# One GpSimd chain for the factors of both normalisations, and the residual's moments ahead of the first remainder

## The reference, cut to what matters

```python
x = x + attn(layernorm(x))     # linear attention with decay in 4 heads; attn returns its input + reads @ W_read.T
x = x + ffn(layernorm(x))      # 8 experts, the best 2 for each token, F = 1024, gelu

def layernorm(x):              # without gain and offset
    m, v = mean(x, -1), var(x, -1)
    return (x - m) / sqrt(v + 1e-5)
```

## Time and profile before

| | us |
|---|---|
| median of 3 runs (lowest, highest) | 563.22 (561.47, 564.38) |
| the profiled execution | 562.67 |
| its span in the profile | 560.9 |
| TensorE busy in it | 530.1 |
| VectorE busy | 448.4 |
| ScalarE busy | 338.3 |
| GpSimd busy | 246.9 |

### The profile page before, as it was taken

How to read it: one execution, slowest core, us unless ns; L and a number is a source line. 1 busy time by engine, 2 the same in 40 slices (tenths; PEclk the granted TensorE clock), 3 DMA queues, 4 the chain that set the end, 5 groups by cost and what they waited for, 6 DMA issues and landing times.

```text
span 560.9 us, 17645 instructions
## 1 busy us (share of the span) xinstructions
PE 530.1 (95%) x5234; PEld 415.3 (74%) x5234; DVE 448.4 (80%) x1375; ACT 338.3 (60%) x856; POOL 246.9 (44%) x291
## 2 busy tenths in 40 slices
PE   7799899999999999999999999999999999999991
PEld 7677778778786777777777777777777777777770
DVE  4889999999987689868768787688777777778861
ACT  6899989898745876445545554455544544545540
POOL 5625778888746084523223233223322333322433
PEclk9999999999998999999999999999999999999997
DMA  5576867777345396433263364343344454344323
GB/s 161 201 229 225 258 185 234 210 222 231 126 105 129 87 216 101 71 60 62 51 103 56 53 105 77 63 68 61 61 63 79 78 78 75 68 64 67 63 37 36
DMA packets 85096, 63.33 MB, mean 113 GB/s; under 512 B 54224, under 2 KB 77392, under 8 KB 85008
## 3 DMA queue, kind: packets, MB, share of 16 engines
q1 hardware_dynamic: 71328, 43.94, 32.3%
q0 software_dynamic: 13392, 18.27, 17.3%
q10 hardware_dynamic: 288, 0.00, 0.0%
HBM read 37.56 MB, written 24.62 MB: 111 GB/s over the span
## 4 chain that ended last, share of the span: by engine, by line
PE 77%; DVE 10%; issue 4%; DMA 3%; ACT 2%; POOL 1%; SPq 1%; POOLq 0%; DVEq 0%; ACTq 0%
PE psum L1697 32%; PE psum L1712 21%; PE psum L1714 10%; PE psum L1509 3%; DVE weights L874 2%; PE psum L1592 2%; PE psum L1573 2%; PE psum L1599 2%; PE psum L1520 2%; DVE arena L1052 1%; PE psum L1559 1%; DMA arena<-sent_rows 1%; PE psum L1612 1%; PE psum L1496 1%; DVE arena L1063 1%
## 5 line engine op out<-in xcount | busy, mean ns | idle before, releaser
L1697 PE MATMUL psum<-arena,weights 128*128 128x256 f16 (+1 forms) x2208 | 279.7, 249 | 1.1 <-DVE arena L1316 1.0
L1697 PEld LDWEIGHTS psum<-arena,weights 128*128 x2208 | 187.4, 98 | 79.3 <-issue 4.1
L589 POOL DMA_INDIRECT out<-arena,tile_in x71 | 115.0, 1619 | 233.4 <-DVE arena L1343 126.9
L1712 PE MATMUL psum<-weights,arena 128*128 x556 | 211.7, 381 | 0.0
L826 ACT ACTIVATE arena<-psum,b_cur 128x256 f32<-128x256 f32 (+1 forms) x368 | 131.4, 423 | 129.9 <-PE psum L1697 115.6
L1714 PE MATMUL psum<-weights,arena 128*128 x556 | 152.0, 273 | 0.0
L1327 DVE TENSOR_TENSOR arena<-arena 128x512 f16<-128x512 f32 x142 | 98.5, 694 | 10.8 <-ACT arena L843 6.3
L559 POOL DMA_INDIRECT sent_rows<-arena,tiny x64 | 65.4, 1022 | 35.5 <-issue 17.8
L1323 DVE CAST arena<-arena 128x512 f16<-128x512 f32 x126 | 53.5, 424 | 8.8 <-ACT arena L826 8.5
L1712 PEld LDWEIGHTS psum<-weights,arena 128*128 128x128 f16 x556 | 54.4, 98 | 5.0
L1714 PEld LDWEIGHTS psum<-weights,arena 128*128 128x128 f16 x556 | 54.5, 98 | 4.6
(11 more groups left out here) (199 smaller groups left out, 642.9 us busy)
## 6 DMA issues: line engine op xcount, KB each, us to landing
weights<-in_experts SPq DMA_DIRECT2D x32, 512.0 KB, 4.8
arena<-sent_rows SPq DMA_DIRECT2D x100, 64.0 KB
arena<-in_b SPq DMA_DIRECT2D x46, 128.0 KB, 3.2
arena<-in_x SPq DMA_DIRECT2D x16, 256.0 KB, 3.4
out<-arena SPq DMA_DIRECT2D x16, 256.0 KB, 4.1
arena<-sent_rows SPq DMA_DIRECT2D x84, 32.0 KB
sent_rows<-pad SPq DMA_DIRECT2D x7, 265.0 KB, 4.6
tile_in<-sent_rows SPq DMA_DIRECT2D x71, 4.5 KB, 2.6
```

Of the source, the lines that this page charges most:

```text
L589: pool.indirect_dma_start(out=out, out_offset=bass.IndirectOffsetOnAxis(ap=at_u, axis=0), in_=yout[:, u % 4], in_offset=None, compute_op=A ...
L1697: last = pe.matmul(ps_h[:, f % 2, mm * n:(mm + 1) * n], w1_of(e_of[i], k, lo, per * (f - GROUP[i]) + mm), turned[:, i % 2, part, k, 0:n], ...
L1712: pe.matmul(to, h_hi[:, z % 4, at], w2_of(e_of[t], m), start=(m == 0), stop=(m == MF - 1), skip_group_check=True)
```

## The change

GpSimd's loop over the two kinds of normalisation becomes one chain of four operations over both, on 128x4 numbers: `moments_all`, `variances`, `factors` and `shifts` hold the columns of chunk n beside those of chunk n-3. The chain begins when the moments of both are there. In steps 0 to 2 and 16 to 18, where one kind alone is there, it runs over two columns. ScalarE's two normalisations wait for the same semaphore, `shifts_done`. VectorE makes the residual's statistics and moments directly behind the residual's addition, ahead of the first remainder.

```diff
@@ GpSimd, step(n)
-                for lag, moments, ve, rs, shift, got, mid, end, last, used, ago in (
-                        (0, moments1, ve1, rs1[par], shift1[par], "moments1_done", "ve1_done", "rs1_done",
-                         "shift1_done", "res_done", 1),
-                        (3, moments2, ve2, rs2, shift2, "moments2_done", "ve2_done", "rs2_done", "shift2_done",
-                         "xm_done", 0)):
-                    if active(n, lag):
-
-                        m = n - lag
-                        reached(pool, got, m)
-                        reached(pool, used, m - ago - 1)
-                        pool.tensor_scalar(ve, moments[:, :, 1], EPS, None, ALU.add)
-                        pool.tensor_scalar(shift, moments[:, :, 0], -1.0, None, ALU.mult).then_inc(S[mid], 1)
-                        reached(pool, mid, m)
-                        pool.tensor_tensor(rs, ve, minus_half[:].to_broadcast([P, B]), ALU.pow).then_inc(S[end], 1)
-                        reached(pool, end, m)
-                        pool.tensor_tensor(shift, shift, rs, ALU.mult).then_inc(S[last], 1)
+                if active(n, 0) or active(n, 3):
+                    both_kinds = slice(0 if active(n, 0) else B, 2 * B if active(n, 3) else B)
+                    count = both_kinds.stop - both_kinds.start
+                    if active(n, 0):
+
+                        reached(pool, "moments1_done", n)
+                        reached(pool, "res_done", n - 2)
+                    if active(n, 3):
+
+                        reached(pool, "moments2_done", n - 3)
+                        reached(pool, "xm_done", n - 5)
+                    got, ve = moments_all[:, both_kinds], variances[:, both_kinds]
+                    rs, shift = factors[par][:, both_kinds], shifts[par][:, both_kinds]
+                    pool.tensor_scalar(ve, got[:, :, 1], EPS, None, ALU.add)
+                    pool.tensor_scalar(shift, got[:, :, 0], -1.0, None, ALU.mult).then_inc(S["taken"], 1)
+                    reached(pool, "taken", n)
+                    pool.tensor_tensor(rs, ve, minus_half[:].to_broadcast([P, count]),
+                                       ALU.pow).then_inc(S["factors_done"], 1)
+                    reached(pool, "factors_done", n)
+                    pool.tensor_tensor(shift, shift, rs, ALU.mult).then_inc(S["shifts_done"], 1)
@@ ScalarE, normalise(m) and chunk_normalise(m)
-                reached(a, "shift2_done", m)
+                reached(a, "shifts_done", m + 3)
...
-                reached(a, "shift1_done", m)
+                reached(a, "shifts_done", m)
@@ VectorE, step(n)
                 if active(n, 3):
                     residual(n - 3)
+                if active(n, 3):
+                    residual_stats(n - 3)
+                    residual_moments(n - 3)
                 for j in splits(n)[0:1]:
                     split_low(j)
-                if active(n, 3):
-                    residual_stats(n - 3)
                 if active(n, 5):
                     weigh_gates(n - 5)
-                if active(n, 3):
-                    residual_moments(n - 3)
                 if active(n, 2):
                     weigh_scores(n - 2)
```

More of the change, by code:

```diff
@@ L227, in build @@
         stats1 = by_batch(small(B * 6))
-        moments1 = by_batch(small(B * 2))
-        rs1, shift1, gain1 = ([small(B) for _ in range(2)] for _ in range(3))
-        ve1 = small(B)
+        moments_all = small(2 * B * 2).rearrange("p (c e) -> p c e", e=2)
+        moments1, moments2 = moments_all[:, 0:B], moments_all[:, B:2 * B]
+        variances = small(2 * B)
+        factors, shifts = ([small(2 * B) for _ in range(2)] for _ in range(2))
+        rs1, shift1 = ([half[:, 0:B] for half in kind] for kind in (factors, shifts))
+        gain1 = [small(B) for _ in range(2)]
+        rs2_of = lambda m: factors[(m + 3) % 2][:, B:2 * B]
+        shift2_of = lambda m: shifts[(m + 3) % 2][:, B:2 * B]
         stats2 = by_batch(small(B * 6))
-        moments2 = by_batch(small(B * 2))
-        ve2, rs2, shift2 = small(B), small(B), small(B)
         logit = by_batch(small(B * E))
@@ L290, in build @@
         S = {n: sem(n) for n in (
-            "stats1_done", "moments1_done", "ve1_done", "rs1_done", "shift1_done", "gain1_done", "xn_done", "xT_ps", "xT_done", "xcol_done", "xlo_done",
+            "stats1_done", "moments1_done", "taken", "factors_done", "shifts_done", "gain1_done", "xn_done", "xT_ps", "xT_done", "xcol_done", "xlo_done",
             "res_done", "keys_done", "queries_done", "val_ps", "val_done", "score_ps", "score_done",
             "read_ps", "read_done", "state_ps", "state_done", "proj_ps",
-            "x1_done", "stats2_done", "moments2_done", "ve2_done", "rs2_done", "shift2_done", "xm_done",
+            "x1_done", "stats2_done", "moments2_done", "xm_done",
             "mT_ps", "mT_done", "logit_ps", "logit_done", "top_done", "top_at_done", "shifted_done", "exp_done",
@@ L672, in normalise @@
                 for b in range(B):
-                    last = a.activation(row[:, m % ROWS, b, 0:D], res_of(m)[:, b], ACT.Identity, scale=rs2[:, b:b + 1],
-                                        bias=shift2[:, b:b + 1])
+                    last = a.activation(row[:, m % ROWS, b, 0:D], res_of(m)[:, b], ACT.Identity, scale=rs2_of(m)[:, b:b + 1],
+                                        bias=shift2_of(m)[:, b:b + 1])
                 last.then_inc(S["xm_done"], 1)
@@ L881, in moments @@
                 reached(v, "stats1_done", n)
-                reached(v, "ve1_done", n - 1)
+                reached(v, "taken", n - 1)
                 for b in range(B):
@@ L997, in residual_moments @@
                 reached(v, "stats2_done", m)
-                reached(v, "ve2_done", m - 1)
+                reached(v, "taken", m + 2)
                 for b in range(B):
@@ L1373, in first_normalise @@
                 s = m % 2
-                reached(v, "shift1_done", m)
+                reached(v, "shifts_done", m)
                 for b in range(B):
```

## The result

The changed kernel takes 564.9 us (median of 20 runs, 562.28 to 568.19). The kernel before takes 562.41 us beside it (20 runs, 559.72 to 564.8). The ratio is 1.005, with a 95% interval of 1.0028 to 1.0072, so the change costs between 1.6 and 4.1 us. The forecast was 4.1 us slower (567.3 against 563.22), with an inner case B of 1.8 us. The measured 2.5 us (medians) to 2.8 us (ratio) lies between the two. The interval does not include 1, but the size is at the border of the 2.8 us that the prediction took as its own limit for telling a difference.

A forecast was written before the change was run, and what follows sets the result against it. The first stage was taken as bound by operation order on near-full engines, shifting the end one for one. Terms +1.10 (step 3), +0.96, +0.62, +1.23, +0.17 sum to +4.1 on 563.22: 567.3 us, range 562.8 to 571.0.

The forecast's parts named there:

- case B: Rival, first stage: the power costs the same on four columns, VectorE's 9.61 us sets the step; +1.8, 565.0 us; chance 0.32.
- the exposed waits: VectorE: residual statistics and moments each wait for the operation right before, 0.32 us a step; +0.96 over steps 5 to 8.
- step 3: Step without gates or places: VectorE's later splits come early, GpSimd's last multiply loses the port; +1.10 us, all carried.
- ScalarE's loop over the joint chain: ScalarE's two normalisations wait for GpSimd's one chain; 9.91 us a loop, above VectorE's 9.61 with two weight pieces.
- the power: GpSimd's L549 in the joint chain: 0.72 us on two columns, taken as 0.52 us longer on four.
- the collision: GpSimd's last multiply, started just behind VectorE's L874 split, ends only with it: 1.14 us instead of 0.20 before the change.
- The two-piece steps: First-stage steps with two weight pieces, from step 8 on: 9.91 us forecast, set by ScalarE, against VectorE's 9.61.
- 8 to 9: First stage, from step 8's residual addition to step 9's: 9.91 instead of 9.29 us, +0.62.
- the six steps: First stage, from step 9's residual addition to step 15's: 59.46 instead of 58.23 us, +1.23.
- the three-piece steps: First-stage steps with three weight pieces, 5 to 8: VectorE without a gap sets them, 10.74 us forecast against 10.42 before.
- C: Rival: GpSimd's last multiply loses the port to the second split every step, 11.16 us each; +15.3, 578.6 us; chance 0.13.
- D: Rival: dependent waits and longer power cost nothing, VectorE's 9.29 us sets two-piece steps; -1.8, 561.4 us; chance 0.10.

## Why the prediction was right, and where it was off

The mechanism held: the exposed waits, the lost port in step 3 and ScalarE's loop over the joint chain are all in the trace. The sum of 4.1 us was too large by some 1.7, most of it for one term, the power, and a dip of the clock gave back 0.4 of that. That the time came out slower than before is the mechanism; how near it came out is in part luck.

**The exposed waits** (3 x 0.32 us): right. The undisturbed steps take 10.76 and 10.75 against 10.74 forecast, the gaps are 0.11 and 0.03 us, and the kernel with the gates in the gap got 0.17 us back. The Trainium skill's page VectorE: DVE Perf Modes, section The DRAIN you can't avoid, has a semaphore in a chain of copies cost nothing extra. Here the runs show that two operations which wait for the one right before them cost 0.32 us a step more than where others stand between.

**Step 3** (+1.10 us): right in mechanism, 0.16 us too much. The product was asked for at 28.25, 0.49 us behind the remainder's start, and ended 0.09 us behind the first of the two, as forecast. Both ways of taking the collision away gave most of the step back: 9.63 us with the remainders held, 9.39 us with the short power.

**The power on four columns** (1.24 us): the mis-sized term. It is 1.04 us: I took the upper of two bounds, the whole surplus of 0.52 us paid again for two more columns, and 0.32 of it is paid, 0.16 us a column. The lower bound, nothing, was off by more. By the measured value the same sum of the prediction gives 4.93 - 0.20 + 0.03 + 1.10 + 1.00 + 2.85 = 9.71 us, and 9.69 us was measured.

**The two-piece steps** follow from that: 8 to 9 costs 0.40 instead of 0.62, and the six steps 0.03 instead of 1.23. ScalarE does set them, as forecast, by 0.07 us over VectorE.

**The sum.** With the measured terms it is 0.94 + 0.99 + 0.40 + 0.03 = 2.4 us, and the clock dip in the third of the three-piece steps makes it 2.77. The medians give 2.5, the ratio of the runs 2.8. Of the forecast 4.1 us, 1.4 were too much for the power (0.22 at 8 to 9, 1.20 in the six steps), 0.2 too much for step 3, and 0.2 too much for the last step: L719 was to come 0.17 us later behind step 15's addition and comes 0.06 us earlier (6.83 against 6.89 us).

**The rivals.** B had the wrong price for the power and nearly the right steps (9.61 against 9.69): its 1.8 us is 0.7 to 1.0 us from the measured difference, nearer than the forecast's 4.1, which is 1.3 to 1.6 away. C did not occur in steps 5 on. The margin forecast at 0.18 us was 92.11 - 91.70 = 0.41 us at the product's start, and the new chain alone shows what C costs when the margin is gone. D fell with the gaps. What none of the cases had is that the dip of the clock falls in another place from one execution to the next, and can hide 1.7 us in a pair of profiles.

**The port.** The Trainium skill's page SBUF — State Buffer, section SBUF: two separate sides, says that of VectorE with two inputs in SBUF and GpSimd, the one that starts first holds the shared pair for its whole instruction. The traces agree: a product that started 0.10 to 0.18 us behind the remainder took 0.9 to 1.0 us longer, one that started 0.21 to 0.44 us ahead of it took its 0.2 us.

## What to carry to other kernels

Two chains that are joined begin with the later of their inputs, so look first at when each input is there, and only then at the instructions saved: 2.3 us less work on GpSimd in 20 bought nothing. Where a short operation of one engine stands near a long one of another that takes the same port, write down both start times: the order of two starts 0.1 us apart is worth 1 us, and moving a short chain into a gap that is there anyway (here between two scatters) brought the other one 0.2 us ahead of the long operation. And a gain made by taking out slack has to be measured on more than one chip: the same kernel gave 0.9973, 1.0055 and 1.0049.

## What the runs showed of the hardware that I had not expected

- GpSimd's power on 128 partitions takes 0.39 us and 0.157 us for each column (704 ns on 2, 5411 ns on 32), the product 0.19 to 0.23 us on all of these.
- A dip of the granted clock to between 0.5 and 0.8 in a stretch of 5 us is in the first 200 us of every trace here, at 70 us in one and at 175 us in another. One cost 0.4 us in a step of the changed kernel; two steps of the kernel with the new order alone took 11.1 and 11.2 us with one, where the two-piece steps behind them took 9.6 to 10.3.
- Chips differ: 562, 575 and 572 us for the same kernel, with the single operations of the first stage as long on all of them. The loss is in waits between engines, and its cause is open.
